# A twelve-stage decoder on one core: packs issued later, MLP halves reordered, ternary pairs issued further ahead

## The chip, the cores and the metric

One core of a Trainium2 chip runs the whole program in one launch. The metric is the device time of an execution in microseconds (us); the number of a kernel is the median of its runs.

## The reference, cut to what matters

The input x has 8 sequences of 128 tokens of 128 numbers; a context of the same shape goes into the cross attentions. Twelve layers, each with a layer norm ahead and an addition behind, follow one another. The change touches the first three, and where the context is turned:

```python
x = x + _L0_attn_ref(_layernorm(x), Wq, Wkv, null_kv, Wout)
x = x + _L0_xattn_ref(_layernorm(x), ctx_1024, Wk, bk, Wq, bq, Wv, bv, W1, b1, W2, b2)
x = x + _L0_ffn_ref(_layernorm(x), w_gate, w_up, w_down)
```

The first is an attention with 16 heads of 64 that share one set of keys and values and have one extra key that is a parameter. The second is an attention whose values come from the context, followed by an MLP (128 to 512, GELU, 512 to 128). The third is a gated MLP whose weights are rounded to -1, 0 and 1 times their mean size, and whose inputs are quantised to 8 bits by row:

```python
scale = 127.0 / clip(max(abs(x), axis=-1), 1e-05)         # of a row
xq    = clip(round(x * scale), -128, 127) / scale
y     = bitlinear(silu(bitlinear(x, w_gate)) * bitlinear(x, w_up), w_down)
```

## The kernel before, in words

Each engine has its own list of instructions, and semaphores order them across engines. A stage is a block: all engines meet at its end. Within a block an engine works strictly in the order written, so the order of the calls in each engine's function is the schedule. x stays on the chip as eight tiles of 128 tokens; a "half" is four of them. Where a stage can, it already begins the layer norm of the next stage (`ahead`): moments on VectorE, `rstd` by a power on GpSimd, scaling on VectorE.

The opening block (`turn_context`, line 155) issues all transfers on SP's queue: constants, x, the context, then the early packs of weights in the order of the stages (lines 164 to 168). TensorE turns the context by eight transposes (176), ScalarE keeps it (183), VectorE makes small tables from the constants after a wait for x (188).

The first attention (`multi_query_attention`, 277) starts with GpSimd, which waits for the weights (345), builds rows of the extra key (346 to 348) and only then inverts the variances (350). TensorE multiplies these rows by the output weights (437), turns the normalised x (440), and makes queries, keys and values (364, 374). Then 32 units of four heads run in a pipeline over `s` (459): project the heads of an earlier pair of units (429), scores (397), mix (418), turn (408). Mixes and projections share bank 7: `mix(m)` waits for the addition (560) of an earlier projection by line 416, `project(h)` by line 425.

The cross attention with its MLP (`attention_with_mlp`, 1050) has the MLP in a block of its own: eight matmuls up (1072), ScalarE's GELU (1091), matmuls down by half (1080), VectorE's addition by half (1099). On VectorE, `TernaryWeights` (1112) prepares the next stage's weights; its average over partitions is a matmul ahead of the sixth matmul up (1071).

The ternary stage (`ternary_ffn`, 1835) works on halves for quantising (1957) and on pairs of tiles for the rest: hidden rows (1880, 1881) into two banks for gate and two for up, SiLU on ScalarE (1926), multiply on VectorE (1979), peaks (1985), scale on ScalarE (1935), round on VectorE (1996), transposes (1892), a copy on ScalarE (1943), projection (1901), addition (2001). `build` (3760) places the weights in three regions and lists which packs are loaded early.

Of the kernel before, what the change touches and what calls it, by code (L numbers as in the profile page):

```python
# [28 lines left out]
HALF = 512  # L29
# [125 lines left out]
def turn_context(nc, g, loads):  # L155

    with Stage(nc, "context") as st:
        ctx = st.sb("ctx", [T, B, D])
        loaded, turned = st.sem("loaded"), st.sem("turned")
        with nc.Block() as block:  # L160
# [9 lines left out]
            @block.tensor  # L170
            def _(pe):
                pe.wait_ge(g.const.loaded, 16)
                pe.wait_ge(loaded, 16)
                for half in range(2):
                    for j in range(4):
                        last = nc.tensor.transpose(g.bank[half][:, j * T:(j + 1) * T], ctx[:, 4 * half + j, :], g.ident)
                    last.then_inc(turned, 1)

            @block.scalar
            def _(act):  # L180
                for half in range(2):
                    act.wait_ge(turned, half + 1)
                    nc.scalar.activation(g.ctxT[:, half * HALF:(half + 1) * HALF], g.bank[half][:], ACT.Copy)

            @block.vector
            def _(dve):
                dve.wait_ge(g.const.loaded, 16)
                dve.wait_ge(g.x_loaded, 16)
# [88 lines left out]
def multi_query_attention(nc, g, w, st):  # L277
# [18 lines left out]
    tps, oT_bank, out_bank = bank[6], bank[7][:, 0:2 * T], bank[7][:, 2 * T:3 * T]  # L296
# [10 lines left out]
    def part(i):  # L307

        return bank[4 + i % 4]

# [25 lines left out]
    with nc.Block() as block:  # L336
        @block.sync
        def _(sp):
            start_loads(sp, st.loads, [])
# [20 lines left out]
        def _(pe):  # L360
# [50 lines left out]
            def mix(m):  # L411
# [3 lines left out]
                if m >= 3:  # L415
                    pe.wait_ge(added, (m - 1) // 2)
# [5 lines left out]
            def project(h):  # L422
                pe.wait_ge(oT_kept, min(2 * h + 3, UNITS))
                if h >= 1:
                    pe.wait_ge(added, h)
                for m in (2 * h, 2 * h + 1):
                    for j in range(2):
                        pair = 2 * (m % 4) + j
                        last = nc.tensor.matmul(out_bank, oT[:, m % 4, j * T:(j + 1) * T],
# [28 lines left out]
            make_values(VAL1, 1)  # L458
            for s in range(2, UNITS + 6):
                if s % 2 == 1 and 0 <= s - 7:  # L460
                    project((s - 7) // 2)
# [6 lines left out]
                if s == 32:  # L468
                    pe.wait_ge(exped, 30)
                    ahead.turn(pe, 0, bank[4])  # L470

        @block.scalar
        def _(act):
# [39 lines left out]
            for s in range(2, UNITS + 2):  # L513
# [4 lines left out]
                if s == 32:  # L518
                    ahead.keep(act, 0, bank[4])

        @block.vector
        def _(dve):
# [35 lines left out]
            def add(h):  # L558
                dve.wait_ge(projected, h + 1)
                nc.vector.tensor_tensor(g.x[:, h // 2, :], g.x[:, h // 2, :], out_bank, ALU.add).then_inc(added, 1)  # L560

            norm.take_moments(dve, 0)
# [487 lines left out]
def attention_with_mlp(nc, g, w, st):  # L1050
# [7 lines left out]
    ternary = TernaryWeights(nc, g, st)  # L1058
    with nc.Block() as block:
# [5 lines left out]
        def _(pe):  # L1065
            for m in range(2 * NJ):
# [3 lines left out]
                if m == 5:  # L1070
                    ternary.average(pe, bank[7])
                nc.tensor.matmul(bank[m % 6][:], w["w1"][:, j * 128:(j + 1) * 128],
                                 oT[:, half * HALF:(half + 1) * HALF], start=True, stop=True).then_inc(up, 1)
            for b in range(B):
                if b % 4 == 0:
                    pe.wait_ge(kept, NJ * (b // 4 + 1))
                if b == 4:
                    pe.wait_ge(ternary.unit_ready, 1)
                for j in range(NJ):
                    last = nc.tensor.matmul(bank[6 + b // 4][:, (b % 4) * D:(b % 4 + 1) * D],  # L1080
                                            hid[:, j, b * T:(b + 1) * T], w["w2"][:, j * D:(j + 1) * D],
                                            start=(j == 0), stop=(j == NJ - 1))
                if b % 4 == 3:
                    last.then_inc(down, 1)
# [10 lines left out]
        def _(dve):  # L1095
# [11 lines left out]
            ahead.take_moments(dve, 0)  # L1107
            add(1)
    g.norm_rooted = 1


class TernaryWeights:
# [20 lines left out]
    def round_weights(self, dve, bank):  # L1133
# [11 lines left out]
        nc.vector.tensor_scalar(self.g.ternary_wq[:], wf[:], 1.0, -1.0, ALU.min, ALU.max)  # L1145

# [688 lines left out]
def ternary_ffn(nc, g, w, st):  # L1835
# [5 lines left out]
    peak, inv = st.sb("peak", [T, B]), st.sb("inv", [T, B])  # L1841
    gate_scale, up_scale = st.sb("gate_scale", [T, B]), st.sb("up_scale", [T, B])
    hf, hq, hqT = st.sb("hf", [T, B, D]), st.sb("hq", [T, B, D], BF16), st.sb("hqT", [D, TOK], BF16)
# [4 lines left out]
    quantised, h_turned, hqT_kept, hidden, silu_ready, prod_ready, inverted, scaled, rounded, prod_turned, prodT_kept, made, added = (  # L1848
        st.sem(s) for s in ("quantised", "h_turned", "hqT_kept", "hidden", "silu_ready", "prod_ready", "inverted", "scaled",
# [3 lines left out]
    with nc.Block() as block:  # L1853
# [5 lines left out]
        def _(pool):  # L1859
            norm.invert(pool, 0)  # L1860
            norm.invert(pool, 1)
            ahead.invert(pool, 0)

        @block.tensor
        def _(pe):
            def turn_rows(half):
                pe.wait_ge(quantised, half + 1)
# [88 lines left out]
        def _(dve):  # L1956
            def quantise_rows(half):
                b = slice(4 * half, 4 * half + 4)
                dve.drain()
                nc.vector.tensor_reduce(peak[:, b], g.h[:, b, :], X, ALU.max, apply_absolute_value=True)  # L1960
                dve.drain()
                nc.vector.tensor_scalar(peak[:, b], peak[:, b], 1e-5, 1.0 / 127.0, ALU.max, ALU.mult)
                dve.drain()
                nc.vector.reciprocal(inv[:, b], peak[:, b])
                nc.vector.tensor_scalar(gate_scale[:, b], peak[:, b], unit[:, 0:1], None, ALU.mult)
                nc.vector.tensor_scalar(up_scale[:, b], peak[:, b], unit[:, 1:2], None, ALU.mult)
                dve.drain()
                nc.vector.tensor_tensor(hf[:, b, :], g.h[:, b, :], bc(inv[:, b], 2, D), ALU.mult)
                dve.drain()
                nc.vector.tensor_scalar(hf[:, b, :], hf[:, b, :], ROUND, ROUND, ALU.add, ALU.subtract)  # L1970
                dve.drain()
                nc.vector.tensor_scalar(hq[:, b, :], hf[:, b, :], 127.0, -128.0, ALU.min, ALU.max).then_inc(quantised, 1)

# [39 lines left out]
            for q in range(PAIRS):  # L2013
                round_products(q)
                if q + 1 < PAIRS:
                    find_peaks(q + 1)
                if q + 2 < PAIRS:
                    multiply(q + 2)
                if q == PAIRS - 1:
                    ahead.take_moments(dve, 0)  # L2020
                if q < PAIRS - 1:
                    add(q)
            ahead.scale(dve, 0)
            add(PAIRS - 1)
# [1735 lines left out]
def build(nc, dram, out, layouts, first=0, last=12):  # L3760
# [12 lines left out]
    g.in_group, g.corner_bf = sb("in_group", [128, 4], F32), sb("corner_bf", [128, 32], BF16)  # L3773
    g.mask_loaded, g.bias_loaded = nc.alloc_semaphore("mask_loaded"), nc.alloc_semaphore("bias_loaded")
# [10 lines left out]
    g.bias_rows = g.region_a[0:32, 7168:7296]  # L3785
    g.mask_parts = g.region_a[:, 0:2048].bitcast(BF16).rearrange("p (b c k) -> p b c k", b=B, c=4)
# [37 lines left out]
    turn_context(nc, g, [(packs[n], dram[n]) for n in early])  # L3824
# [179 lines left out]
```

## Time and profile before

| what | value |
|---|---|
| median of 3 runs | 1343.27 us (1342.66 to 1344.61) |
| the profiled execution's own time | 1342.8 us |
| its span, first to last instruction | 1341.0 us |
| mean granted clock of TensorE | 0.904 |
| TensorE busy | 1116.9 us, 83% |
| VectorE busy | 775.2 us, 58% |
| ScalarE busy | 660.2 us, 49% |
| GpSimd busy | 332.5 us, 25% |

The profile calls TensorE PE (PEld for its weight loads), VectorE DVE, ScalarE ACT, GpSimd POOL and SyncE SP. A timeline row gives the start and the duration in us, engine, line, operation, what is written and read, the shape, the count of instructions merged into the row, and in brackets the idle time of the engine before it with what ended that. L12 is line 12 of the kernel. An fp32 matmul shows as two records. The names of stages are cut: L_attn, L_xattn and L_ffn stand for any layer's. A granted clock of 1.00 is TensorE's full speed.

### The profile page before, as it was taken

How to read it: one execution, taken by the hardware profiler on the slowest of the kernel's cores; microseconds unless marked ns; L12 is line 12 of the kernel's file. 1: busy time of each engine (PE TensorE's matmuls, PEld its weight loads, DVE VectorE, ACT ScalarE, POOL GpSimd, SP SyncE). 2: the span in 40 equal slices, each digit the busy share in tenths (PEclk: the TensorE clock that was granted, in tenths of full speed). 3: DMA queues.
4: the chain of work that ended last, by engine and by line, in shares of the span. 5: the costliest groups of instructions: out<-in, count | busy, mean ns of one | idle time of the engine just before them, and what ended most of it. 6: DMA issues, size and time to landing. Idle time of an engine off the chain costs nothing. (4 is left out here: it accounts for less than half of the span.)

```text
span 1341.0 us, 25706 instructions
## 1 busy us (share of the span) xinstructions
PE 1116.9 (83%) x9898; PEld 721.7 (54%) x9899; DVE 775.2 (58%) x1948; ACT 660.2 (49%) x1386; POOL 332.5 (25%) x320
## 2 busy tenths in 40 slices
PE   6898784598889975779869865979889988798998
PEld 4565563346666642347527634847434444475776
DVE  4565546586665478867886786546362565453111
ACT  2564343463452245777686662535656443345332
POOL 1333200023210026464564520240000034700000
PEclk9999897599899977869978995889899989899999
DMA  7000000200000000000000000080196710000000
GB/s 304 1 2 2 1 3 0 97 0 1 3 1 1 1 1 0 1 2 1 1 1 2 1 0 1 2 339 14 31 193 127 159 17 1 2 3 1 1 0 16
DMA packets 18329, 44.83 MB, mean 33 GB/s; under 512 B 4992, under 2 KB 8096, under 8 KB 17568
## 3 DMA queue, kind: packets, MB, share of 16 engines
q1 hardware_dynamic: 18208, 43.20, 11.2%
q8 instruction: 79, 1.29, 0.4%
q14 instruction: 42, 0.34, 0.1%
HBM read 42.41 MB, written 0.79 MB: 32 GB/s over the span
## 5 line engine op out<-in xcount | busy, mean ns | idle before, releaser
L930 ACT ACTIVATE L_xattn_pT<-banks 128x512 f32<-128x512 f32 x128 | 69.0, 598 | 87.9 <-PE banks L808 87.9
L241 POOL TENSOR_TENSOR norm_rstd<-norm_var,norm_power 128x4 f32<-128x4 f32 x24 | 24.6, 1026 | 345.9 <-DVE norm_var L234 345.8
L991 DVE TENSOR_REDUCE L_xattn_top<-banks 128x4 f32<-128x512 f32 x128 | 79.5, 684 | 36.3 <-PE banks L776 36.3
L1576 DVE TENSOR_TENSOR L_ffn_a<-L_ffn_a,L_ffn_share 128x512 f32<-128x512 f32 x64 | 39.9, 685 | 61.0 <-DMA L_ffn_share<-L_ffn_shares 60.6
L1803 ACT ACTIVATE L_ffn_aT<-banks,L_ffn_shift 128x512 f32<-128x512 f32 x64 | 43.3, 687 | 58.9 <-PE banks L1755 57.3
L1490 PE MATMUL banks<-L_ffn_a,region_a 128*128 128x512 f32 x136 | 67.5, 601 | 5.1 <-DVE L_ffn_a L1576 5.1
L1816 DVE SCALAR_TENSOR_TENSOR x<-banks,L_ffn_combine,x 128x128 f32<-128x128 f32 x64 | 18.0, 344 | 88.7 <-PE banks L1766 88.7
L1481 PE MATMUL banks<-hT,region_a 128*128 128x512 f32 x136 | 68.8, 611 | 0.0
L1766 PEld LDWEIGHTS banks<-region_b,L_ffn_aT 128*128 128x128 f32 x512 | 59.4, 192 | 6.7 <-issue 6.7
L490 ACT ACTIVATE L_attn_p<-banks,L_attn_shift 128x129 f32<-128x129 f32 x128 | 45.4, 369 | 33.0 <-DVE L_attn_shift L540 33.0
L1755 PE MATMUL banks<-hT,region_b 128*128 128x512 f32 x128 | 59.6, 609 | 0.0
L1766 PE MATMUL banks<-region_b,L_ffn_aT 128*128 128x128 f32 x512 | 59.6, 275 | 0.0
L1537 ACT ACTIVATE L_ffn_a<-banks 128x512 f32<-128x512 f32 x68 | 40.7, 599 | 36.8 <-PE banks L1481 36.7
L1645 PE MATMUL banks<-hT,region_a 128*128 128x512 f32 x128 | 57.7, 594 | 1.3 <-PEq L78 1.3
L2995 POOL TENSOR_TENSOR L_attn_rstd<-L_attn_ssum,L_attn_power 128x4 f32<-128x4 f32 x24 | 24.2, 1010 | 125.9 <-DVE L_attn_ssum L3628 125.9
L354 POOL TENSOR_TENSOR L_attn_p<-L_attn_p,L_attn_inv 128x512 f32<-128x512 f32 x32 | 33.3, 1040 | 74.0 <-DVE L_attn_inv L544 74.0
L1685 ACT ACTIVATE L_ffn_act_out<-banks 128x512 f32<-128x512 f32 x32 | 19.1, 597 | 56.9 <-PE banks L1645 56.8
L3050 PE MATMUL banks<-hT,region_b 128*128 128x512 f32 x64 | 39.6, 765 | 8.3 <-DVE region_b L3583 6.3
L1490 PEld LDWEIGHTS banks<-L_ffn_a,region_a 128*128 128x128 f32 x136 | 25.8, 192 | 37.9 <-issue 26.6
L1481 PEld LDWEIGHTS banks<-hT,region_a 128*128 128x128 f32 x136 | 26.7, 197 | 33.0 <-issue 30.5
L1541 ACT ACTIVATE L_ffn_a<-L_ffn_a 128x512 f32<-128x512 f32 x68 | 42.6, 628 | 0.0
L250 DVE TENSOR_SCALAR h<-x,norm_moments,norm_rstd 128x128 f32<-128x128 f32 x96 | 33.2, 476 | 14.3 <-POOL norm_rstd L241 12.7
(546 smaller groups left out, 2890.8 us busy)
## 6 DMA issues: line engine op xcount, KB each, us to landing
L_ffn_share<-L_ffn_shares SPq DMA_DIRECT2D x32, 512.0 KB, 10.8
region_b<-in_L_ffn SPq DMA_DIRECT2D x1, 6216.0 KB, 30.1
region_a<-in_L_ffn SPq DMA_DIRECT2D x1, 4416.0 KB, 13.2
region_b<-in_L_attn SPq DMA_DIRECT2D x1, 3150.5 KB, 10.5
region_a<-in_L_ffn SPq DMA_DIRECT2D x1, 3080.5 KB, 21.2
region_b<-in_L_attn SPq DMA_DIRECT2D x1, 1633.5 KB, 9.1
region_b<-in_L_xattn SPq DMA_DIRECT2D x1, 835.0 KB, 9.7
w_tables<-in_tables SPq DMA_DIRECT2D x1, 832.0 KB, 12.6
```

Of the source, the lines that this page charges most:

```text
L490: last = nc.scalar.activation(p[:, s % 4, i, 0:T + 1], bank[k + a][:, j * W:j * W + T + 1], ACT.Exp, bias=shift[:, s % 4, i:i + 1], scale= ...
L930: nc.scalar.activation(pT[:, n % 2, 4 * i:4 * i + 4, :], rows_of(flip[i][:], 4), ACT.Exp, scale=scale).then_inc(exped, 1)
L991: nc.vector.tensor_reduce(top[:, 32 * i:32 * i + 32:HD], rows_of(score[i][:], 4), X, ALU.max).then_inc(topped, 1)
L1481: nc.tensor.matmul(up[k % 4][:], w["up"][:, tile * 128:(tile + 1) * 128], g.hT[:, half * HALF:(half + 1) * HALF], start=True, stop=True).t ...
L1490: nc.tensor.matmul(out[half][:], w["down"][:, tile * D:(tile + 1) * D], a[:, k % AHEAD, :], start=(k % PER_HALF == 0), stop=(k % PER_HALF ...
L1537: nc.scalar.activation(a[:, k % AHEAD, :], up[k % 4][:], ACT.Relu).then_inc(relued, 1)
L1541: nc.scalar.activation(a[:, k % AHEAD, :], a[:, k % AHEAD, :], ACT.Square).then_inc(squared, 1)
L1576: nc.vector.tensor_tensor(a[:, k % AHEAD, :], a[:, k % AHEAD, :], share[:, batch % RING, j, :], ALU.mult).then_inc(weighed, 1)
L1645: nc.tensor.matmul(up[j][:], w["up"][:, at:at + 128], g.hT[:, half * HALF:(half + 1) * HALF], start=True, stop=True).then_inc(hidden, 1)
L1755: nc.tensor.matmul(up[j][:], w["up"][:, at:at + 128], g.hT[:, half * HALF:(half + 1) * HALF], start=True, stop=True).then_inc(hidden, 1)
L1766: last = nc.tensor.matmul(out[u][:, b * D:(b + 1) * D], aT[:, u, j, b * T:(b + 1) * T], w["down"][:, at:at + D], start=(j == 0), stop=(j = ...
L1803: nc.scalar.activation(aT[:, u, j, :], up[j][:], ACT.Gelu, bias=shift[:, TILES * ex + j:TILES * ex + j + 1]).then_inc(activated, 1)
```

## The change

The opening block issues only the constants, x and the first pack; its transposes, its ScalarE copies and its wait for x are gone. The seven other early packs and the context are issued on SP's queue in the first attention, the context after the packs of the second and third stage. The context is turned by TensorE at steps 33 and 34 of the attention's pipeline and kept by ScalarE behind its last step.

In that attention the last three projections write to banks 5, 2 and 3 and wait for the exponentials that free these, not for additions; the last mixes wait for addition 13 at most; projection 14 stands behind mix 31.

In the MLP's block the average moves ahead of the fourth matmul up, and the first half is brought down before the last three matmuls up. VectorE there also normalises and quantises the first half of the ternary stage's rows (a new class `QuantisedRows`).

In the ternary stage the multiplication that scales the second half's rows goes to GpSimd, both first pairs' hidden rows and SiLUs stand ahead of the second half's turning, SiLU of pair q+2 stands behind scale of pair q, and VectorE's order is written out. The diff, cut to its core:

```diff
-def turn_context(nc, g, loads):
+def begin(nc, g, loads):
...
-                sp.dma_start(ctx[:], g.dram["ctx_1024"].rearrange("b t d -> t b d")).then_inc(loaded, 16)
-                for pack, source in loads:
-                    sp.dma_start(pack.tile, source).then_inc(pack.loaded, 16)
+                sp.dma_start(loads[0][0].tile, loads[0][1]).then_inc(loads[0][0].loaded, 16)
...
+    LAST_OUT = {13: 5, 14: 2, 15: 3}
+    def out_bank(h):
+        return bank[LAST_OUT[h]][:, 0:D] if h in LAST_OUT else bank[7][:, 2 * T:3 * T]
...
-            start_loads(sp, st.loads, [])
+            start_loads(sp, st.loads[:2], [])
+            sp.dma_start(g.ctx, g.dram["ctx_1024"].rearrange("b t d -> t b d")).then_inc(g.ctx_loaded, 16)
+            start_loads(sp, st.loads[2:], [])
...
                 if m >= 3:
-                    pe.wait_ge(added, (m - 1) // 2)
+                    pe.wait_ge(added, min((m - 1) // 2, 13))
...
             def project(h):
-                pe.wait_ge(oT_kept, min(2 * h + 3, UNITS))
-                if h >= 1:
-                    pe.wait_ge(added, h)
+                if h in LAST_OUT:
+                    pe.wait_ge(oT_kept, 2 * h + 2)
+                    pe.wait_ge(exped, (30, 32, 32)[h - 13])
+                else:
+                    pe.wait_ge(oT_kept, 2 * h + 3)
+                    if h >= 1:
+                        pe.wait_ge(added, h)
...
+                if s == 33:
+                    turn_context(0)
+                if s == 34:
+                    turn_context(1)
+                if s == 35:
+                    project(14)
+                if s == 37:
+                    project(15)
...
+            raise_to(0)
+            raise_to(1)
+            raise_to(2)
+            ternary.average(pe, bank[7])
+            raise_to(3)
+            raise_to(4)
+            bring_down(0)
+            raise_to(5)
+            raise_to(6)
+            raise_to(7)
+            bring_down(1)
...
             add(0)
             dve.drain()
             ahead.take_moments(dve, 0)
+            ahead.scale(dve, 0)
+            rows.find_peaks(dve, 0)
+            dve.drain()
+            nc.vector.tensor_tensor(rows.hf[:], g.h[:, 0:4, :], bc(rows.inv[:, 0:4], 2, D), ALU.mult)
+            dve.drain()
+            rows.round(dve, 0)
             add(1)
...
-            norm.invert(pool, 0)
             norm.invert(pool, 1)
+            rows.scale(pool, 1)
             ahead.invert(pool, 0)
...
             turn_rows(0)
             make_hidden(0)
+            make_hidden(1)
             turn_rows(1)
-            make_hidden(1)
             for q in range(PAIRS):
-                turn_products(q)
                 if q + 2 < PAIRS:
                     make_hidden(q + 2)
+                turn_products(q)
                 project(q)
...
             silu(0)
+            silu(1)
             keep_rows(1)
             for q in range(PAIRS):
                 scale(q)
-                if q + 1 < PAIRS:
-                    silu(q + 1)
+                if q + 2 < PAIRS:
+                    silu(q + 2)
                 keep_products(q)
...
-            norm.take_moments(dve, 0)
-            norm.scale(dve, 0)
-            quantise_rows(0)
             norm.take_moments(dve, 1)
             norm.scale(dve, 1)
+            rows.find_peaks(dve, 1)
             multiply(0)
+            dve.wait_ge(rows.scaled, 1)
+            rows.round(dve, 1)
             find_peaks(0)
-            quantise_rows(1)
             multiply(1)
...
+            round_products(0)
+            find_peaks(1)
+            multiply(2)
+            round_products(1)
+            find_peaks(2)
+            add(0)
+            multiply(3)
+            round_products(2)
+            find_peaks(3)
+            add(1)
+            round_products(3)
+            dve.drain()
+            ahead.take_moments(dve, 0)
+            add(2)
             ahead.scale(dve, 0)
-            add(PAIRS - 1)
+            add(3)
```

## Rows read from the trace of the kernel before

**Rows 1.** Timeline of the start (columns as told above)

```profile
5.59 0.23 DVE L189 CAST ident_bf<-w_const 128x128 bf16<-128x128 f32 x1 [5.59 <-DMA x<-in_x]
...
7.56 1.94 PE L176 MATMUL banks<-w_const,context_ctx 128*128 128x128 f32 x8 [7.56 <-DMA context_ctx<-in_ctx]
...
11.41 0.21 POOL L346 TENSOR_TENSOR L_attn_kvT<-region_b 128x8 f32<-128x8 f32 x1 [0.28 <-DMA region_b<-in_L_attn]
...
12.27 3.75 PE L437 MATMUL banks<-region_b,L_attn_null_wide 128*128 128x128 f32 x16 [2.77 <-POOL L_attn_null_wide L348]
...
15.81 1.06 PE L259 MATMUL banks<-w_const,h 128*128 128x128 f32 x4
...
17.56 1.98 PE L364 MATMUL banks<-hT,region_b 128*128 128x512 f32 x4 [0.69 <-ACT hT L476]
```

**Rows 2.** Timeline of the end of the first attention

```profile
122.58 1.11 PE L429 MATMUL banks<-region_b,L_attn_oT 128*128 128x128 f32 x8
...
128.18 0.65 PE L418 MATMUL banks<-L_attn_pT,L_attn_kv 128*64 128x256 f32 x4 [0.47 <-DVE x L560]
...
128.87 0.42 DVE L556 COPY L_attn_oT<-banks 128x256 f32<-128x256 f32 x1 [0.84 <-PE banks L418]
...
129.35 1.16 PE L429 MATMUL banks<-region_b,L_attn_oT 128*128 128x128 f32 x8 [0.52 <-DVE L_attn_oT L556]
...
130.54 0.29 DVE L560 TENSOR_TENSOR x<-x,banks 128x128 f32<-128x128 f32 x1 [1.25 <-PE banks L429]
```

**Rows 3.** Ternary stage: busy us of PE, PEld, DVE, ACT, POOL; clock; DMA; GB/s

```profile
214.00:256.00 42.00, 14.59 (x87) 8.38 (x88) 28.78 (x83) 17.04 (x28) 2.01 (x2) 0.56 0.00 1
```

**Rows 4.** Timeline of the ternary stage

```profile
215.14 1.28 ACT L1945 ACT_TABLE_LOAD   x1 [8.17 <-PEq L78]
...
215.18 1.11 DVE L250 TENSOR_SCALAR h<-x,norm_moments,norm_rstd 128x128 f32<-128x128 f32 x4 [1.07 <-PEq L78]
...
219.17 0.43 DVE L1972 TENSOR_SCALAR L_ffn_hq<-L_ffn_hf 128x512 bf16<-128x512 f32 x1
...
220.31 0.60 ACT L1919 ACTIVATE L_ffn_hqT<-banks 128x512 bf16<-128x512 bf16 x1 [3.67 <-PE banks L1869]
...
234.29 0.68 DVE L1996 TENSOR_SCALAR L_ffn_prodq<-L_ffn_prodf 128x1024 bf16<-128x1024 f32 x1
...
235.06 1.22 DVE L1985 TENSOR_REDUCE L_ffn_peak<-L_ffn_prod 128x2 f32<-128x1024 f32 x1
...
236.80 1.33 ACT L1935 ACTIVATE L_ffn_prodf<-L_ffn_prod,L_ffn_inv 128x512 f32<-128x512 f32 x2
...
238.04 1.24 ACT L1926 ACTIVATE L_ffn_gated<-banks,L_ffn_gate_scale 128x512 f32<-128x512 f32 x2
...
238.82 1.41 DVE L1979 SCALAR_TENSOR_TENSOR L_ffn_prod<-banks,L_ffn_up_scale,L_ffn_gated 128x512 f32<-128x512 f32 x2 [1.92 <-ACT L_ffn_gated L1926]
...
250.90 0.69 DVE L1996 TENSOR_SCALAR L_ffn_prodq<-L_ffn_prodf 128x1024 bf16<-128x1024 f32 x1 [0.36 <-ACT L_ffn_prodf L1935]
...
255.23 0.60 DVE L2001 SCALAR_TENSOR_TENSOR x<-banks,L_ffn_out_scale,x 128x128 f32<-128x128 f32 x2
```

**Rows 5.** Transfers of the first 40 us: KB each, us from issue to landing

```profile
region_b<-in_L_attn SPq DMA_DIRECT2D x1, 1633.5 KB, 9.1
```

**Rows 6.** Timeline of the MLP

```profile
196.08 7.36 PE L1072 MATMUL banks<-L_xattn_oT,region_b 128*128 128x512 f32 x10 [0.63 <-PEq L653]
...
206.08 7.31 PE L1080 MATMUL banks<-region_b,L_xattn_ks 128*128 128x128 f32 x64
...
209.85 0.69 DVE L1099 TENSOR_TENSOR x<-x,banks 128x512 f32<-128x512 f32 x1 [2.40 <-PE banks L1080]
...
212.26 1.01 POOL L241 TENSOR_TENSOR norm_rstd<-norm_var,norm_power 128x4 f32<-128x4 f32 x1 [58.75 <-DVE norm_var L234]
...
213.42 0.69 DVE L1099 TENSOR_TENSOR x<-x,banks 128x512 f32<-128x512 f32 x1 [1.24 <-PE banks L1080]
```

**Rows 7.** The page's costliest groups, GpSimd's multiplication of 128x512

```profile
L354 POOL TENSOR_TENSOR L_attn_p<-L_attn_p,L_attn_inv 128x512 f32<-128x512 f32 x32 | 33.3, 1040 | 74.0 <-DVE L_attn_inv L544 74.0
```

More of the change, by code:

```diff
@@ L152, in start_loads @@
         sp.wait_ge(pack.loaded, 16)
-def turn_context(nc, g, loads):
[L157 to L160, printed above, removed]
+def begin(nc, g, loads):
+    with nc.Block() as block:
             @block.sync
@@ L295, in multi_query_attention @@
     bank = g.bank
[L296 removed]
+    ctx_turned = st.sem("ctx_turned")
+    tps, oT_bank = bank[6], bank[7][:, 0:2 * T]
+    LAST_OUT = {13: 5, 14: 2, 15: 3}
     KV0, VAL0, KV1, VAL1 = 1, 7, 12, 21
@@ L458, in _, with turn_context @@
             make_values(VAL1, 1)
+            def turn_context(half):
+                if half == 0:
+                    pe.wait_ge(g.ctx_loaded, 16)
+                    pe.wait_ge(exped, 31)
+                for j in range(4):
+                    last = nc.tensor.transpose(bank[half][:, j * T:(j + 1) * T], g.ctx[:, 4 * half + j, :], g.ident)
+                last.then_inc(ctx_turned, 1)
             for s in range(2, UNITS + 6):
-                if s % 2 == 1 and 0 <= s - 7:
+                if s % 2 == 1 and 0 <= s - 7 < UNITS - 4:
                     project((s - 7) // 2)
@@ L519, in _ @@
                     ahead.keep(act, 0, bank[4])
+            for half in range(2):
+                act.wait_ge(ctx_turned, half + 1)
+                nc.scalar.activation(g.ctxT[:, half * HALF:(half + 1) * HALF], bank[half][:], ACT.Copy)
         @block.vector
@@ L1057, in attention_with_mlp @@
     ahead = Norm(nc, g, st, ahead=True)
-    ternary = TernaryWeights(nc, g, st)
+    ternary, rows = TernaryWeights(nc, g, st), QuantisedRows(nc, g, st)
     with nc.Block() as block:
@@ L1065, in _, with raise_to @@
         def _(pe):
-            for m in range(2 * NJ):
+            def raise_to(m):
                 j, half = m % NJ, m // NJ
@@ L1069, in _, with bring_down @@
                     pe.wait_ge(kept, m - 5)
-                if m == 5:
-                    ternary.average(pe, bank[7])
                 nc.tensor.matmul(bank[m % 6][:], w["w1"][:, j * 128:(j + 1) * 128],
                                  oT[:, half * HALF:(half + 1) * HALF], start=True, stop=True).then_inc(up, 1)
[L1074 to L1077, printed above, removed]
+            def bring_down(half):
+                pe.wait_ge(kept, NJ * (half + 1))
+                if half == 1:
                     pe.wait_ge(ternary.unit_ready, 1)
[L1079 to L1084, printed above, removed]
+                for b in range(4 * half, 4 * half + 4):
+                    for j in range(NJ):
+                        last = nc.tensor.matmul(bank[6 + half][:, (b % 4) * D:(b % 4 + 1) * D],
+                                                hid[:, j, b * T:(b + 1) * T], w["w2"][:, j * D:(j + 1) * D],
+                                                start=(j == 0), stop=(j == NJ - 1))
+                last.then_inc(down, 1)
+            raise_to(0)
[9 more added lines that the diff above has]
+            bring_down(1)
         @block.scalar
@@ L1145, in round_weights, with __init__, find_peaks, scale @@
         nc.vector.tensor_scalar(self.g.ternary_wq[:], wf[:], 1.0, -1.0, ALU.min, ALU.max)
+class QuantisedRows:
+    def __init__(self, nc, g, st):
+        self.nc, self.g = nc, g
+        self.peak, self.inv, self.gate_scale, self.up_scale = (g.row_scales[:, i, :] for i in range(4))
+        self.hf, self.hq = st.sb("hf", [T, 4, D]), g.row_quants
+        self.inverted, self.scaled, self.quantised = (st.sem(s) for s in ("row_inverted", "row_scaled", "quantised"))
+    def find_peaks(self, dve, half):
+        nc, g, unit = self.nc, self.g, self.g.ternary_unit
+        b = slice(4 * half, 4 * half + 4)
+        dve.drain()
+        nc.vector.tensor_reduce(self.peak[:, b], g.h[:, b, :], X, ALU.max, apply_absolute_value=True)
+        dve.drain()
+        nc.vector.tensor_scalar(self.peak[:, b], self.peak[:, b], 1e-5, 1.0 / 127.0, ALU.max, ALU.mult)
+        dve.drain()
+        nc.vector.reciprocal(self.inv[:, b], self.peak[:, b]).then_inc(self.inverted, 1)
+        nc.vector.tensor_scalar(self.gate_scale[:, b], self.peak[:, b], unit[:, 0:1], None, ALU.mult)
+        nc.vector.tensor_scalar(self.up_scale[:, b], self.peak[:, b], unit[:, 1:2], None, ALU.mult)
+    def scale(self, pool, half):
+        b = slice(4 * half, 4 * half + 4)
+        pool.wait_ge(self.inverted, 1)
+        self.nc.gpsimd.tensor_tensor(self.hf[:], self.g.h[:, b, :], bc(self.inv[:, b], 2, D), ALU.mult).then_inc(self.scaled, 1)
+    def round(self, dve, half):
+        nc = self.nc
+        nc.vector.tensor_scalar(self.hf[:], self.hf[:], ROUND, ROUND, ALU.add, ALU.subtract)
+        dve.drain()
+        nc.vector.tensor_scalar(self.hq[:, 4 * half:4 * half + 4, :], self.hf[:], 127.0, -128.0, ALU.min,
+                                ALU.max).then_inc(self.quantised, 1)
 class SoftmaxRouter:
@@ L1866, in turn_rows @@
             def turn_rows(half):
-                pe.wait_ge(quantised, half + 1)
+                if half == 1:
+                    pe.wait_ge(rows.quantised, 1)
                 for j in range(4):
@@ L1956, in _ @@
         def _(dve):
[L1957 to L1972, printed above, removed]
             def multiply(q):
@@ L3823, in build @@
     packs["tables"] = g.tables
-    turn_context(nc, g, [(packs[n], dram[n]) for n in early])
+    begin(nc, g, [(packs[n], dram[n]) for n in early[:1]])
+    late[run[0][0]] = early[1:]
     tables_from = next((name for name, _ in run if name in [n for n, _ in STAGES[3:]]), None)
```

45 lines of the change are left out of this document (13 added, 32 removed).

## The prediction

> **What bounds the kernel now.** I read the timeline of the first 30 us, that of the end of the first attention, the busy times of the ternary stage and its timeline, the list of transfers, and the MLP. From 256 us on nothing is edited, and I take it to move as a block. Times are on the clock of the trace of before.
>
> At the start, x has landed when VectorE begins at 5.59, the context when TensorE begins at 7.56, the first attention's pack when GpSimd's null rows begin at 11.41 [rows 1]: one after the other, in the order of issue. The attention waits for the last of these. GpSimd makes the null rows, TensorE multiplies them (12.27 to 16.02), the transposes of h follow, and the queries start at 17.56.
>
> At the end of that attention a mix waits for the addition of the projection before it ("0.47 <-DVE x L560"), since both use bank 7: mix, copy, project, add, one after the other [rows 2].
>
> In the ternary stage, 214 to 256, VectorE is busy 28.8 of 42 us, ScalarE 17.0, TensorE 14.6, at a mean granted clock of 0.56 [rows 3]. No engine is full; a chain that goes from one to the next sets the time. One turn of it [rows 4]: round 0.68, peaks until the inverse is there (235.06 to 236.80), scale 1.33, SiLU 1.24, multiply 1.41 (half beside the SiLU), add 0.60, round.
>
> **The change, part by part.**
>
> (a) Start. The context's 512 KB and its eight transposes leave the path, and the later packs are issued behind them on SP's queue, in the attention. The pack took 11.41 - 7.56 = 3.85 behind the context; right behind x it lands at 5.59 + 3.85 = 9.44. Gain 7.56 - 5.59 = 1.97, say **2.0**. From below: at the pack's own rate (1633.5 KB in 3.85 us, 424 KB per us [rows 5]) 512 KB are worth 1.2. From above: the pack is also issued about 0.5 sooner, 2.5. I take the context's own time, since that transfer is what is removed. The rest of the opening hides in this: GpSimd waits for the pack ahead of inverting the variances, and VectorE's moments can start at 5.6. SP has nothing else to issue; the seven packs and the context flow during the queries, and none is needed before 124.
>
> (b) Tail of the attention. The last three projections get banks of their own, so mix 29 doesn't wait for addition 13, nor mix 31 for addition 14. By engine order, with the steps of [rows 2]: projection 13 at 122.5 to 123.65; mix 29 at 123.5; turn 31; four context transposes, 0.45 of issue; mix 30 at 125.1; four transposes; copy of mix 30 to 126.2; mix 31 at 126.3 instead of 128.18. But VectorE's order is still add 14, then the copy of mix 31: projection 14 ends at 127.95, add 14 at 128.28, copy 128.3 to 128.7, projection 15 at 128.75 instead of 129.35. The end goes from 130.83 to 130.24: **0.6**. Between 0.3 (handovers 0.05 longer) and 0.9 (transposes free). ScalarE's two context copies lie in its idle time before the block's end; uncovered they cost 1.2. Were the transposes as slow as at the start (1.94 for eight [rows 1]), mix 31 would be 0.9 later and the gain lost.
>
> (c) MLP. TensorE spends 196.08 to 203.44 on the first five matmuls [rows 6]. The average now stands ahead of the fourth, some 0.2, so the first half is brought down from 203.6, and the 3.75 that this takes (206.08 to 209.83) end at 207.35: VectorE's addition starts 2.5 sooner. Rounding the weights follows the average, so it moves forward too and is out of the way. Then VectorE does more than before: to GpSimd's start 2.41 (209.85 to 212.26), GpSimd 1.01, then normalising and quantising the first half, which took 215.18 to 219.60 in the next block [rows 4], 4.42. That ends at 215.25; the second addition 0.69: 215.9, against 214.11. The block is **1.8 longer**. TensorE isn't late: the three matmuls left are six records of 0.43 (the step at 17.56 [rows 1]), to 209.95, the Gelu 0.7, bringing down 3.75: 214.4, covered by 0.8 of VectorE's chain; without that cover the block would end with it, at 215.1.
>
> (d) Ternary stage, from 216.95 (215.14 plus 1.8). Its first rows are ready, so ScalarE's table load is first: 1.28 and 0.2, and the rows are kept at 218.45 against 220.31. VectorE: moments 1.7, GpSimd 1.0, normalising and peaks 2.65 (the 4.42 less a multiplication of 0.69, two roundings of 0.43 and gaps): 222.3. First multiply to 223.7. Beside it GpSimd scales the second half's rows: its multiplications of this size take 1.04 [rows 7], to 223.2, before they are wanted. Below, VectorE's own 0.69 saves nothing; above, twice 1.04, beside a busy VectorE, costs 0.5. I take 1.04. Rounding the rows 0.95, peaks 1.75 to the inverse, at 226.45; scale 1.33 to 227.8, second multiply to 228.0. The first round starts at 228.0 against 234.29: **6.3 ahead**, mostly since the second pair's hidden rows no longer wait for the second half's quantising.
>
> The loop. SiLU of pair q+2 now follows scale of pair q, one turn sooner, and leaves the chain. What is left is round 0.68, 1.75 to the inverse, keeping the products (about 1.1, partly beside), scale 1.33. Followed by engine the rounds start at 228.0, 232.45, 237.05 and 240.85: three turns in 12.85, where they took 250.90 - 234.29 = 16.61, **3.75 more**. VectorE with 0.68, 1.85, 1.41 and 0.60, 4.5 a turn, is then nearly the bound. After the last round the new order (moments, addition, normalising, addition) takes 5.1 against 4.93 (to 255.83). The stage ends at 245.95 instead of 255.83: **9.9**, with the 1.8 paid.
>
> ScalarE's table now stands ahead of everything here. The row shows 1.28 from 215.14, and the traced rows are kept long after, at 220.31; in these rows the load itself is the whole price. The Trainium skill, page ScalarE: Activation LUTs, section What ACT_TABLE_LOAD costs, gives a drain of about 1.38 on top; by it the rows would be kept at 219.8, and the sum be 1.4 smaller. No row here shows that drain.
>
> **Sum.** 2.0 + 0.6 + 9.9 = 12.5. The profiled execution took 1342.8 (span 1341.0): 1330.3. The median shown, 1343.27, is 0.5 above it: **1330.8**.
>
> **Rivals.**
> 1. The loop keeps its turn: hidden rows still need the banks that multiply frees, so an earlier SiLU only moves the wait. Then 3.75 is lost: 1334.6. For it: only two banks each for gate and up. Against it: VectorE multiplies ahead of the round, with some 2 us in hand. 12%.
> 2. TensorE stays slow longer at the start. The null products are 16 records in 3.75 us, 0.23 each, and four transposes took 1.06, while the 512-wide records at 17.56 are 0.43 apart; ten such records of the MLP took 7.36, so most were about 0.85 apart there. TensorE was thus at its lower level (1.2 GHz) until about 17. The context's transposes no longer come ahead of it. If the rise comes ten records later, 10 x 0.42 = 4.2 are lost: 1335.0. Against it: the null products are a busy stretch of their own, and an idle gap lay between. 10%. The Trainium skill, page TensorE: Matmul & The Clock Gate, section What's actually happening, calls the slow state the default that activity releases, which speaks for this rival; no trace here has the start without those transposes.
> 3. ScalarE is held once more as long as the load itself, 1.28, after the table load of the ternary stage; the rows would not show it, as ScalarE waited anyway: 1332.1. 5%.
> 4. Slower: the clock of rival 2, not given at all during the queries. Eighteen matmuls of two records, at 0.85 instead of 0.43, cost 15.1, more than the 12.5: 1345.9. It decides from 36 records; from 24 on the gain is under 2.7. Against it: in the MLP 7.36 us held both levels, so the rise came within about 6 us of matmuls. 3%.
> 5. The edits do nothing, since other waits stand in the same places: 1343. The new banks and TensorE's order make that hard to see. 2%.
>
> **How the numbers follow.** The forecast has 68%. Its own range: (a) 1.2 to 2.5, (b) 0.3 to 0.9, (c, d) 8.4 to 11 (handovers of 0.05 missed, or TensorE at its upper level in part of the ternary stage), and 1 us either way for when the clock rises in the stages behind. Rivals 1 to 3 reach to 1335.0. Range 1328.0 to 1335.3. Faster by over 0.2% (2.7 us, about what a measurement of this kernel can tell) takes in the forecast and rivals 1 to 3: 0.95; within 0.2%, rival 5: 0.02; slower, rival 4: 0.03.
>
> **What would show it.** GpSimd's null rows at about 9.4; the last addition of the first attention 2.6 sooner; the MLP's block 1.8 longer, with its last step bound by VectorE; the ternary block 29 us instead of 41; rounds 4 to 4.6 apart, and multiply's wait for SiLU (1.92 at 238.82) gone. It is wrong if a round waits on a multiply that waits on SiLU, if the queries' records at the start are 0.85 apart, or if what lies behind 256 doesn't simply move along.

## The result, and the profile after

The changed kernel takes 1337.42 us (median of 20 runs, 1333.08 to 1347.40) beside 1347.76 for the kernel before (20 runs, 1340.93 to 1354.40): a ratio of 0.9932, 95% interval 0.9915 to 0.9948, so 9.2 us faster (7.0 to 11.5). The forecast was 1330.8 in 1328.0 to 1335.3. The sign was right; time and range were not. Two things lie in the 6.6 us between: the median forecast from (1343.27, three runs) was 4.5 below that of twenty, and a gain of 12.5 (a ratio of 0.9907) was forecast where the ratio gives 9.2 and the two medians 10.3.

The profiled execution took 1336.17 (span 1334.4, mean granted clock 0.904 as before). Its span is 6.6 shorter. How far this trace is ahead of that of before, at marks that both have:

| mark | before | after | ahead |
|---|---|---|---|
| last addition of the first attention ends | 130.83 | 132.48 | -1.65 |
| MLP begins | 196.04 | 196.76 | -0.72 |
| ternary stage begins | 215.14 | 216.51 | -1.37 |
| the stage behind it begins | 256.66 | 245.78 | 10.88 |
| 16th load of a table | 527.28 | 516.29 | 10.99 |
| 17th | 562.30 | 553.22 | 9.08 |
| 22nd | 894.62 | 886.91 | 7.71 |
| end of the span | 1341.0 | 1334.4 | 6.6 |

In this pair of traces the whole gain is made in the ternary stage; the start and the MLP are behind, and 4.4 us go again in stages that nobody edited.

Timeline of the start, after:

```profile
10.47 0.21 POOL L335 TENSOR_TENSOR L_attn_kvT<-region_b 128x8 f32<-128x8 f32 x1 [5.11 <-DMA region_b<-in_L_attn]
...
11.33 3.75 PE L430 MATMUL banks<-region_b,L_attn_null_wide 128*128 128x128 f32 x16 [11.33 <-POOL L_attn_null_wide L337]
14.88 1.06 PE L238 MATMUL banks<-w_const,h 128*128 128x128 f32 x4
16.62 3.76 PE L353 MATMUL banks<-hT,region_b 128*128 128x512 f32 x4 [0.69 <-ACT hT L485]
20.20 0.63 PE L238 MATMUL banks<-w_const,h 128*128 128x128 f32 x4
...
25.16 0.70 DVE L550 TENSOR_REDUCE L_attn_top<-banks 128x4 f32<-128x516 f32 x1 [0.45 <-PE banks L386]
```

The null rows begin at 10.47 against 11.41 [rows 1], 0.94 sooner where 1.97 was forecast. Then the first four records of the queries take 3.76 instead of 1.98 [rows 1], some 0.85 apart instead of 0.43, and the start's lead is gone: the first maxima of the scores begin at 25.16 against 24.31. By mix 28 (123.03 below, 120.88 before) this trace is 2.15 behind, so another 1.3 went in between. Over all traces that way took 96.6, 96.6 and 99.1 with the old opening and 96.9 to 99.4 with the new one, so the 1.3 lies within the scatter.

Timeline of the end of the first attention, after:

```profile
123.03 0.65 PE L407 MATMUL banks<-L_attn_pT,L_attn_kv 128*64 128x256 f32 x4 [0.31 <-issue]
...
126.79 0.60 PE L457 MATMUL banks<-w_const,region_a 128*128 128x128 f32 x4
...
129.13 1.16 PE L422 MATMUL banks<-region_b,L_attn_oT 128*128 128x128 f32 x8
130.32 0.29 DVE L572 TENSOR_TENSOR x<-x,banks 128x128 f32<-128x128 f32 x1 [1.88 <-PE banks L422]
130.53 0.42 DVE L568 COPY L_attn_oT<-banks 128x256 f32<-128x256 f32 x1
131.00 1.16 PE L422 MATMUL banks<-region_b,L_attn_oT 128*128 128x128 f32 x8 [0.71 <-DVE L_attn_oT L568]
132.19 0.29 DVE L572 TENSOR_TENSOR x<-x,banks 128x128 f32<-128x128 f32 x1 [1.25 <-PE banks L422]
```

From mix 28 (123.03) to the end of the last addition it takes 9.45; before, 120.88 to 130.83, 9.95. (It is 9.94 or 9.95 in all three traces with the old tail, and 9.44 to 9.46 in the six with the new one as it stands.) As forecast, the copy of mix 31 (130.53) still stands behind addition 14 (130.32), and projection 15 behind that copy.

Timeline of the MLP and the first of the ternary stage, after:

```profile
196.80 4.51 PE L1083 MATMUL banks<-L_xattn_oT,region_b 128*128 128x512 f32 x6 [0.63 <-PEq L666]
...
203.17 3.84 PE L1092 MATMUL banks<-region_b,L_xattn_ks 128*128 128x128 f32 x32
...
210.36 3.84 PE L1092 MATMUL banks<-region_b,L_xattn_ks 128*128 128x128 f32 x32 [0.78 <-ACT L_xattn_ks L1114]
...
214.49 0.43 DVE L1207 TENSOR_SCALAR region_a<-L_xattn_hf 128x512 bf16<-128x512 f32 x1
214.83 0.68 DVE L1122 TENSOR_TENSOR x<-x,banks 128x512 f32<-128x512 f32 x1
216.51 1.28 ACT L2008 ACT_TABLE_LOAD   x1 [6.20 <-PEq L78]
...
217.80 0.20 ACT L2008 ACTIVATE L_ffn_table<-w_const 128x1 f32<-128x1 f32 x1
217.91 0.58 ACT L1982 ACTIVATE L_ffn_hqT<-banks 128x512 bf16<-128x512 bf16 x1
```

VectorE's chain ends the block: the second half is down at about 214.2, and its addition (214.83) stands behind the rounding. 196.76 to 216.51 is 0.65 longer than before (19.10).

Timeline of the ternary stage, after: the four rounds, a multiply and the last addition:

```profile
227.24 0.69 DVE L2043 TENSOR_SCALAR L_ffn_prodq<-L_ffn_prodf 128x1024 bf16<-128x1024 f32 x1
...
229.76 1.40 DVE L2026 SCALAR_TENSOR_TENSOR L_ffn_prod<-banks,region_a,L_ffn_gated 128x512 f32<-128x512 f32 x2
...
231.57 0.69 DVE L2043 TENSOR_SCALAR L_ffn_prodq<-L_ffn_prodf 128x1024 bf16<-128x1024 f32 x1 [0.41 <-ACT L_ffn_prodf L1998]
...
235.93 0.68 DVE L2043 TENSOR_SCALAR L_ffn_prodq<-L_ffn_prodf 128x1024 bf16<-128x1024 f32 x1
...
239.81 0.69 DVE L2043 TENSOR_SCALAR L_ffn_prodq<-L_ffn_prodf 128x1024 bf16<-128x1024 f32 x1 [0.77 <-ACT L_ffn_prodf L1998]
...
244.32 0.61 DVE L2048 SCALAR_TENSOR_TENSOR x<-banks,L_ffn_out_scale,x 128x128 f32<-128x128 f32 x2
```

Three turns take 12.57 where they took 16.61 [rows 4], and no multiply waits for a SiLU. The stage takes 29.27 (216.51 to 245.78) instead of 41.52, VectorE busy for most of it:

```profile
216.50:245.78 29.28, 14.67 (x87) 7.99 (x88) 23.79 (x69) 17.17 (x29) 3.08 (x3) 0.59 0.00 1
```

(columns as in [rows 3]).

### The profile page after: what moved, and what is told of

Same layout as the page of the kernel before. It is cut to its first block and busy times, and to the rows that moved or that the text cites. A ratio compares the mean times of both kernels' runs of the same rounds, so it can differ in the third digit from the quotient of the medians.

```text
span 1334.4 us, 25691 instructions
## 1 busy us (share of the span) xinstructions
PE 1123.0 (84%) x9898; PEld 723.0 (54%) x9899; DVE 775.0 (58%) x1947; ACT 660.2 (49%) x1386; POOL 334.3 (25%) x321
## 5 line engine op out<-in xcount | busy, mean ns | idle before, releaser
L1600 ACT ACTIVATE L_ffn_a<-banks 128x512 f32<-128x512 f32 x68 | 40.7, 599 | 37.0 <-PE banks L1544 36.9
## 6 DMA issues: line engine op xcount, KB each, us to landing
region_b<-in_L_attn SPq DMA_DIRECT2D x1, 1633.5 KB, 8.7
```

The costliest lines, as they stand in the source:

```text
L1600: nc.scalar.activation(a[:, k % AHEAD, :], up[k % 4][:], ACT.Relu).then_inc(relued, 1)
```

## The experiments

**Which half of the change carries the gain.** Two kernels, each with one half. `start_tail` has the new opening and tail, and the MLP and the ternary stage of before:

```diff
+            for m in range(2 * NJ):
...
+                if m == 5:
+                    ternary.average(pe, bank[7])
...
-            rows.round(dve, 0)
             add(1)
```

> Only the edits of the first attention and the opening (parts a and b); MLP and ternary stage as before. Theory 'the start gives its gain back to TensorE's clock': the first pack lands about 1 sooner, the first 512-wide records run 0.85 apart as in the changed kernel's trace, and the whole is 0 to 2 us slower than before (ratio 1.000 to 1.0015). Rival, the prediction's parts a and b: 2.6 us faster (0.998). In the trace, the last addition of the first attention at 130.8 to 132.5 under the theory, at 128.2 under the rival.

Measured: 1348.7, ratio 0.9991 (0.9963 to 1.0019), 1.2 us faster with an interval from 5.0 faster to 2.6 slower, which holds both expectations. In its trace the pack lands at 10.14, but the queries' records are 0.43 apart, not 0.85 as the theory had it, and the last addition ends at 129.47, between the two. `mlp_ternary` is the other half, with the opening and the first attention of before:

```diff
-def begin(nc, g, loads):
+def turn_context(nc, g, loads):
...
-                if h in LAST_OUT:
-                    pe.wait_ge(oT_kept, 2 * h + 2)
```

> Only the edits of the MLP and the ternary stage (parts c and d); opening and first attention as before. Theory: these edits carry the whole gain, the next stage starts 10 to 12 us sooner and all behind moves along within what the clock scatters: ratio 0.991 to 0.993. Rival: a part of it is paid back systematically in the stages behind (the changed kernel's trace lost 3.3 us in the delta-rule stage, from 527 to 895): then that stage takes 370.6 again instead of 367.3, and the ratio is 0.994.

Measured: 1337.51, ratio 0.9927 (0.9902 to 0.9951), 9.8 us, though its start was a late one (MLP at 201.54); ternary block 29.27. Nor is anything paid back as the rival had it: from the 16th load to the 22nd this trace takes 368.13, not 370.6. So a gain as large as the whole comes with the MLP and the ternary stage. Of the 2.6 forecast for start and tail nothing can be told from zero by these runs, nor is 2.6 excluded.

**What the clock costs at the start.** `warm_start` lets TensorE turn the identity 28 times while it waits for the first pack (nobody reads the result):

```diff
+            pe.wait_ge(g.const.loaded, 16)
+            for j in range(28):
+                nc.tensor.transpose(bank[0][:, 0:T], g.ident, g.ident)
```

> The changed kernel with 28 transposes of the identity on TensorE while it waits for the first pack; their result is not used. Theory 'clock': the clock rises before the null products, so their 16 records take about 2.0 instead of 3.75 us, the four transposes 0.6 instead of 1.06, the first 512-wide records are 0.43 apart: the first score's maxima at about 21.5 instead of 25.16, and the whole 3 to 4 us faster than the changed kernel (ratio to before 0.990). Rival 'the steps at the start are not the clock's but the transfers' doing (both use the memory at the same time)': null products 3.75 again, and the whole up to 1 us slower than the changed kernel.

Timeline of its start:

```profile
5.28 4.64 PE L429 MATMUL banks<-w_const 128*128 128x128 f32 x28 [5.28 <-PEq L157]
...
11.55 2.02 PE L433 MATMUL banks<-region_b,L_attn_null_wide 128*128 128x128 f32 x16 [1.63 <-POOL L_attn_null_wide L337]
...
13.41 0.60 PE L238 MATMUL banks<-w_const,h 128*128 128x128 f32 x4
14.70 1.98 PE L353 MATMUL banks<-hT,region_b 128*128 128x512 f32 x4 [0.69 <-ACT hT L488]
```

The 16 null records take 2.02 instead of 3.75, the transposes 0.60 instead of 1.06, the queries are 0.43 apart: TensorE is at its upper level (2.4 GHz) from the null products on. The first maximum of scores comes at 21.45, 3.7 sooner than in the changed kernel's trace, though its pack landed 0.2 later. But the changed kernel's trace was a late one. `start_tail`, `held_packs` and `loop_undone` have no such transposes, and still their queries are 0.43 apart and their first maxima come at 23.05, 23.20 and 23.41; against these the transposes bring 1.6 to 2.0. In whole time: 1337.24, ratio 0.9912 (0.9879 to 0.9944); `held_packs`, compared with the same runs of before, gave 1339.41. The difference has the right sign, but the intervals overlap.

**Why the pack lands late: neighbours or itself.** `held_packs` issues the later packs only when the first has landed:

```diff
+            sp.wait_ge(w.loaded, 16)
             start_loads(sp, st.loads[:2], [])
```

> The changed kernel, but SP waits for the first pack before it issues the other seven and the context. Theory 'the later packs, issued at 5.03, share the engines with the first': the first pack lands at about 9.4 instead of 10.47, and all behind it 1 us sooner. Rival 'the first pack lands when it does because of its own rate and the end of its transfer': 10.2 to 10.5 again, the whole the same as the changed kernel within 0.1%; the other packs land 3 to 5 us later, which nothing waits for.

The pack still lands at 10.66, and the whole is 1339.41, ratio 0.9943 (0.9914 to 0.9973). Busy times by stretch show why (the last three columns are granted clock, DMA share, GB/s):

```profile
7.00:8.50 1.50, 0.00 (x0) 0.00 (x0) 1.21 (x9) 0.00 (x0) 0.00 (x0) 1.00 1.02 427
8.50:9.00 0.50, 0.00 (x0) 0.00 (x0) 0.00 (x0) 0.00 (x0) 0.00 (x0) 1.00 0.44 183
9.00:9.50 0.50, 0.00 (x0) 0.00 (x0) 0.00 (x0) 0.00 (x0) 0.00 (x0) 1.00 0.43 183
9.50:10.00 0.50, 0.00 (x0) 0.00 (x0) 0.00 (x0) 0.00 (x0) 0.00 (x0) 1.00 0.25 105
10.00:10.50 0.50, 0.00 (x0) 0.00 (x0) 0.00 (x0) 0.00 (x0) 0.00 (x0) 1.00 0.00 0
```

With nothing behind it, what is left of the pack after 8.50 moves at under half the rate, on part of the 16 engines by the share of 0.44; in finer slices its last bytes move before 9.80 (so the 105 is a slice that is partly empty), and the landing is seen 0.86 later. The tail is the pack's own, and the neighbours don't delay it. `short_pack` leaves 512 KB out of it, a table that no instruction reads:

```diff
-                    ("wqT", column_tiles(i["L0_attn_Wq"].T)), ("null_row", every_row(np.append(null, np.float32(1))))],
+                    ("null_row", every_row(np.append(null, np.float32(1))))],
```

> The changed kernel without the transposed copy of the query weights in the first pack (512 of its 1633.5 KB, read by nothing). Theory 'the last bytes of the pack, on the slowest transfer engines, set its landing': the pack lands with its bytes, 1.2 to 1.8 sooner than 10.47 to 10.69, at 8.8 to 9.4. Rival 'a fixed time from issue': 10.2 or later.

It lands at 9.87, 0.60 sooner than in the changed kernel (0.82 sooner than in `warm_start`): between the two expectations, and less than the 1.2 that 512 KB are at the rate that the prediction took, 1633.5 KB [rows 5] in 3.85 us. But the full pack's own landings scatter from 10.14 to 11.05, so one trace can't tell 0.6 from 1.2; `best` below, with the same short pack, has it at 9.39. One run: 1341.67.

**The loop.** `loop_undone` puts the SiLUs of the last two pairs one turn back:

```diff
-                if q + 2 < PAIRS:
-                    silu(q + 2)
+                if 1 <= q + 1 and q + 1 < PAIRS and q >= 1:
+                    silu(q + 1)
```

> The changed kernel, with SiLU of pairs 2 and 3 put back behind the scale of pair 1 and 2 (one pair ahead only). Theory of the prediction: SiLU and multiply are in the chain again for two turns, so two rounds are 5.8 to 6.4 apart instead of 4.3, and the ternary block (from its table load to the next stage's) takes 32.5 to 33.2 instead of 29.27. Rival: VectorE's written-out order or the missing quantising brought the shorter turn, and the block stays at 29.3.

Timeline of VectorE in its ternary stage:

```profile
225.57 0.69 DVE L2043 TENSOR_SCALAR L_ffn_prodq<-L_ffn_prodf 128x1024 bf16<-128x1024 f32 x1
...
230.41 1.41 DVE L2026 SCALAR_TENSOR_TENSOR L_ffn_prod<-banks,region_a,L_ffn_gated 128x512 f32<-128x512 f32 x2 [2.22 <-ACT L_ffn_gated L1989]
231.74 0.68 DVE L2043 TENSOR_SCALAR L_ffn_prodq<-L_ffn_prodf 128x1024 bf16<-128x1024 f32 x1
...
236.62 1.41 DVE L2026 SCALAR_TENSOR_TENSOR L_ffn_prod<-banks,region_a,L_ffn_gated 128x512 f32<-128x512 f32 x2 [1.76 <-ACT L_ffn_gated L1989]
237.95 0.68 DVE L2043 TENSOR_SCALAR L_ffn_prodq<-L_ffn_prodf 128x1024 bf16<-128x1024 f32 x1
...
241.82 0.69 DVE L2043 TENSOR_SCALAR L_ffn_prodq<-L_ffn_prodf 128x1024 bf16<-128x1024 f32 x1 [0.76 <-ACT L_ffn_prodf L1998]
```

The waits of multiply for SiLU are back, the two rounds behind them are 6.2 apart, and the block takes 32.94: 3.67 more than 29.27. This part of the gain is shown, and its size: the block takes 29.26 to 29.29 in all six traces that have the whole new order. The whole time of its one run, 1337.36, can't show 3.7 us in a spread of 14.

**How much is chance.** `before_again` is the kernel before, unchanged, profiled once more.

> The kernel before once more, unedited, for the scatter of what the change does not touch. Theory 'chance': its MLP block starts up to 6 us away from the 196.04 of the first trace (201.54 was seen with the same opening), and the delta-rule stage's first part takes either about 34.8 or about 36.9. Rival 'each kernel has its own fixed times': 196.0 within 0.3, and 35.0.

It reaches the MLP at 200.09, against 196.04 in the trace that the prediction read; its MLP takes 16.26 against 19.10, its span is 1346.0 against 1341.0. Its first part of the delta-rule stage, from the 16th table load to the 17th, takes 35.01. So the trace of before had an early start by chance. The old opening reached the MLP at 196.04, 200.09 and 201.54 (`mlp_ternary`), the new one, in the kernels whose start is that of the changed kernel or differs from it by one wait, at 196.76, 194.86, 197.29 and 195.10: means 199.2 and 196.0. The first maxima of the scores say the same: 24.31, 26.57 and 27.72 (mean 26.2) with the old opening, 25.16, 23.05, 23.20 and 23.41 (mean 23.7) with the new one. So the pair of traces set the earliest of the old starts beside the latest of the new. By these few traces the start and tail do gain some 3 us, by the runs of `start_tail` 1.2; the size stays open.

**A version that beats both.** `best` is the changed kernel with 22 of those transposes, the short pack, and the copy of mix 31 ahead of addition 14:

```diff
-                if s % 2 == 1 and 0 <= s - 7:
+                if s % 2 == 1 and 0 <= s - 7 and s != 35:
...
+                if s == 35:
+                    add(14)
+                    dve.drain()
```

> The changed kernel with 22 transposes of the identity while TensorE waits for the first pack, the pack without the unread 512 KB, and the copy of mix 31 ahead of addition 14 on VectorE. Theory: null rows about 1.2 sooner, clock up before the null products (2.0 instead of 3.75, and 512-wide records 0.43 apart from the first), the end of the attention 0.5 to 0.8 sooner; the MLP block starts at 190 to 193 where the changed kernel's traces had 194.9 to 197.3; the whole about 5 us faster than the changed kernel, ratio to before 0.988 to 0.991. Rival: what is won at the start is lost in the scatter behind, ratio 0.993.

Timeline of its start, and of the end of its first attention:

```profile
9.39 0.20 POOL L335 TENSOR_TENSOR L_attn_kvT<-region_b 128x8 f32<-128x8 f32 x1 [3.86 <-DMA region_b<-in_L_attn]
...
10.25 2.02 PE L433 MATMUL banks<-region_b,L_attn_null_wide 128*128 128x128 f32 x16 [0.85 <-POOL L_attn_null_wide L337]
...
124.11 2.05 PE L422 MATMUL banks<-region_b,L_attn_oT 128*128 128x128 f32 x16
...
126.20 0.29 DVE L575 TENSOR_TENSOR x<-x,banks 128x128 f32<-128x128 f32 x1 [0.61 <-PE banks L422]
```

1327.2 (1325.25 to 1333.43), ratio 0.9866 (0.9839 to 0.9893), an interval clear of the changed kernel's and better than the 0.988 to 0.991 expected. The last two projections run as one piece: from the first of them to the end of the last addition it takes 2.38 (124.11 to 126.49) instead of 3.35 (129.13 to 132.48). The MLP begins at 191.21, 4.8 ahead of the mean of 196.0. By ratios the whole is 8.9 below the changed kernel (0.0066 of 1347.76); what lies beyond those 4.8 isn't explained. In the traces `best` is 5.0 ahead of the changed kernel at the 17th table load and 9.1 at the 22nd, so the rest came in stages that nobody edited.

## Why the prediction was wrong, by its steps

Most of the miss is the base: the sum starts from 1343.27, the median of three runs, and twenty put it at 1347.76, which is 4.5 of the 6.6. The rest is the gain, forecast too large by 2.1 (medians) to 3.3 (ratio). In it the landing of the first pack, in part (a), and the standstill of all that lies behind 256 came out wrong; (b) and (c, d) came out right.

**(c, d) MLP and ternary stage: right.** 9.9 was forecast, 9.8 measured by `mlp_ternary` (6.6 to 13.2 by its interval); by the pair of traces 12.25 - 0.65 = 11.6. The first round comes 10.73 behind the stage's start (11.05 forecast), three turns take 12.57 (12.85 forecast), from the last round to the end of the last addition 5.12 (5.1 forecast). `loop_undone` shows that the SiLU was what held the turn; rival 1 falls. The MLP's block was to be 1.8 longer and is 0.65 longer in this trace, bound by VectorE as said: the sum took the first five matmuls at the 7.36 of [rows 6], and here TensorE is done with them sooner, 196.80 to 203.17. Such blocks scatter more than that: 16.26, 19.08 and 19.10 with the old order, 18.07 to 20.93 in seven traces with the new one. Their means, 18.15 and 19.80, are 1.65 apart, near the 1.8.

Rival 3 falls too: the load ends at 217.79, ScalarE's next instruction begins at 217.80 and the one that keeps the rows at 217.91. The drain of about 1.38 behind a load, of the Trainium skill's page ScalarE: Activation LUTs, section What ACT_TABLE_LOAD costs, isn't seen here. The trace of before could have settled this: "the rows would not show it" is true of the ternary stage's row alone. At another load ScalarE is busy until 397.54, loads from 397.56 for 1.28 and begins its next instruction at 398.85, and 15 more of its loads look like that.

**(b) Tail: right.** 0.50 against 0.6, the same in every trace.

**(a) Start: the landing was wrong; what that cost in whole time stays open.** The step was "right behind x it lands at 5.59 + 3.85 = 9.44". The 3.85 were the interval between two landings with the context in front, and passed for the pack's own time behind anything. It lands at 10.47 here and at 10.14 to 11.05 in the variants with the full pack behind x, 4.8 to 5.7 behind x. The mean of these five is 10.60; with the context ahead three traces have 11.41, 11.62 and 13.06, mean 12.03. So the landing moved by 0.94 in this pair and by 1.4 between the means, on either side of the bound from below, the 1.2 of 512 KB at the pack's rate, and not by the context's 1.97. `held_packs` shows that the later packs aren't the cause. That the pack's slow tail is all that the 9.44 left out is argued, not shown.

In this pair the rest went to the clock, 1.8 (3.76 instead of 1.98). The queries stood 0.85 apart, which was rival 2's sign, but not for rival 2's reason, that the context's transposes come no longer ahead. The queries of `start_tail`, without these transposes, and of `before_again` and `mlp_ternary`, with them:

```profile
16.30 1.98 PE L353 MATMUL banks<-hT,region_b 128*128 128x512 f32 x4 [0.69 <-ACT hT L485]
```

```profile
17.77 3.78 PE L364 MATMUL banks<-hT,region_b 128*128 128x512 f32 x4 [0.69 <-ACT hT L476]
```

```profile
19.22 3.73 PE L364 MATMUL banks<-hT,region_b 128*128 128x512 f32 x4 [0.69 <-ACT hT L476]
```

The rise comes at a time of its own, between about 15 and 23 in the traces without added work at the start. `warm_start` shows that with work ahead it comes before the null products.

**What lies behind 256 doesn't move as a block: 4.4 us go in this pair of traces.** The prediction took it so ("I take it to move as a block"). Busy times by stretch around the 16th table load, before (525.28 to 529.28) and then after (from 514.29):

```profile
525.28:527.28 2.00, 0.33 (x2) 0.00 (x0) 0.90 (x1) 1.06 (x1) 2.00 (x3) 0.81 0.00 0
527.28:529.28 2.00, 1.66 (x20) 0.84 (x20) 0.09 (x1) 1.98 (x3) 2.00 (x3) 1.00 0.00 0
```

```profile
514.29:516.29 2.00, 0.33 (x2) 0.00 (x0) 0.90 (x1) 1.06 (x1) 2.00 (x3) 0.50 0.00 0
516.29:518.29 2.00, 1.96 (x16) 1.17 (x20) 0.09 (x1) 1.98 (x3) 2.00 (x3) 0.50 0.00 0
...
522.29:524.29 2.00, 2.00 (x4) 0.73 (x3) 0.00 (x0) 0.00 (x0) 0.00 (x0) 0.50 0.00 0
524.29:526.29 2.00, 2.00 (x13) 1.37 (x11) 1.03 (x2) 1.70 (x5) 1.04 (x1) 0.72 0.00 0
```

In the 2 us ahead of the mark every engine does the same (the same busy times and counts), but in the trace of before the clock rises about 1 us ahead of the mark, in that of the changed kernel about 9 us behind it: from this load to the next it takes 35.02 and 36.93. The edits don't fix the value: `warm_start`, which has the whole change, takes 34.73. Yet all five traces at 36.9 (the changed kernel, `held_packs`, `short_pack`, `loop_undone`, `best`) have the whole change, and the four without the whole of it take 34.7 to 35.0 (`before_again` 35.01); ten traces don't rule out that the change makes the longer value likelier. The Trainium skill, page TensorE: Matmul & The Clock Gate, section What's actually happening, says that the moment of the rise varies from run to run, since what watches TensorE doesn't start with the kernel; these rows agree that it varies, by far more than the half microsecond either way that the section gives for its own kernel, and show nothing of the cause. The forecast allowed 1 us either way for all such moments together.

**The bound of a measurement.** That 0.2% is "about what a measurement of this kernel can tell" rested on three runs within 0.15%. Twenty runs spread over 13.5 us, 1%. A range of 7.3 us for the median of such a kernel, set from three runs and one trace, was too narrow: 4.5 of the miss is the base, the 2.1 left the gain's size (12.5 against the 10.3 between the medians). The terms of the sum give a range of 1327.9 to 1335.0, near the one stated; laid from 1347.76 instead, the stated range would have reached to 1339.8 and held the 1337.42.

## What to carry to other kernels

A step gains what its own stage shows only if it doesn't hang on a clock or a landing with a time of its own: ask what TensorE did in the microseconds ahead, and give it some work while it waits. A transfer that must land early should be small; taking away what was in front of this one brought 0.9 to 1.4 us where 2.0 were forecast. Before a wait is made a rival, look for it at the same kind of instruction elsewhere in the trace. And of a single pair of traces compare the edited stages; a difference in stages that nobody touched is first to be taken for scatter, and a base for scatter from more than three runs.

## What the runs showed of the hardware

A transfer of 1633.5 KB with nothing behind it moved at 427 GB/s from 7.0 to 8.5, then at some 183 GB/s until its last bytes at about 9.8 (`held_packs`). At the start of the kernel the granted clock reads 1.00 (in `held_packs`'s rows above even while TensorE does nothing), yet records of 128x128 are 0.23 apart and those of 128x512 0.85, twice the 0.12 and 0.43 of the upper level; there a column of 1.00 isn't full speed, and the durations tell the level. And the same instructions, after the same instructions, found TensorE at either level, which goes with 1.9 us in one stretch of 35. A table load of ScalarE takes 1.28, and its next instruction begins 0.01 or 0.02 behind it where nothing else is waited for.
